# A decoder block on one core: where the partition maximum of the feed-forward weights and the sums of the skip columns stand

## The reference, cut to what matters

```
x = x + attn(layernorm(x), w_qkv, w_proj)       # 16 heads of 32, causal, ternary weights, 8-bit activations
x = x + mix(layernorm(x), k, skip, ctx, ctx)    # long convolution of products along the 512 columns, 8 x 32 grouping of positions
x = x + ffn(layernorm(x), gate, up, down)       # weights rounded to fp8 (e4m3), silu(gate) * up, then down; scales per column

mix:  kv = v[:, :, :, None, :] * x2[:, :, None, :, :]
      y  = causal_convolution(kv, k) + kv * skip
      out = einsum('bhijl,bhil->bhjl', y, x1)
ffn:  fuse = silu(q(x, gate_w) * gate_scale) * (q(x, up_w) * up_scale);  q(fuse, down_w) * down_scale
```

## Time and profile before

| | |
|---|---|
| median of three runs | 1605.58 us (1601.24, 1605.58, 1606.38) |
| the profiled execution | 1601.21 us, its span 1599.4 us |
| TensorE busy | 1479.1 us, 92% of the span |
| VectorE busy | 1261.7 us, 79% |
| GpSimd busy | 992.7 us, 62% |
| ScalarE busy | 697.4 us, 44% |
| mean granted clock of TensorE | 0.983 of full speed |

### The profile page before, as it was taken

One profiled execution on the slowest core, in us unless ns is written; L12 is line 12 of the kernel. 1 busy time (PEld: TensorE's weight loads), 2 busy tenths in 40 slices (PEclk: granted clock), 3 DMA queues, 4 the chain that ended last, 5 costly groups with the idle time before them and its releaser, 6 DMA issues.

```text
span 1599.4 us, 23982 instructions
## 1 busy us (share of the span) xinstructions
PE 1479.1 (92%) x8967; PEld 839.6 (52%) x9045; DVE 1261.7 (79%) x1841; ACT 697.4 (44%) x1222; POOL 992.7 (62%) x706
## 2 busy tenths in 40 slices
PE   2699999999876787999999999999999999999998
PEld 2477878888752333444444444444444444444443
DVE  5789999999855799888878787788778887878521
ACT  4589999999871103222222222322232223222231
POOL 2389999999973477456545654655645654566242
PEclk9799999999988999999999999999999999999999
DMA  3554645545315112000300210300030020010000
GB/s 135 154 138 132 175 136 148 159 145 144 100 59 184 42 50 77 22 7 14 79 14 9 72 27 0 79 21 7 20 80 7 14 79 14 7 40 1 1 26 27
DMA packets 58708, 105.78 MB, mean 66 GB/s; under 512 B 7625, under 2 KB 11873, under 8 KB 58593
## 3 DMA queue, kind: packets, MB, share of 16 engines
q1 hardware_dynamic: 58400, 104.10, 23.4%
q10 hardware_dynamic: 192, 0.14, 0.1%
HBM read 50.74 MB, written 19.92 MB: 44 GB/s over the span
## 4 chain that ended last, share of the span: by engine, by line
PE 61%; DVE 4%; POOL 2%; issue 1%; ACT 0%; POOLq 0%; DVEq 0%
PE gu L673 21%; PE y L638 10%; PE gu L687 10%; PE y L641 3%; PE y L646 3%; PE y L642 3%; PE gu L626 3%; PE y L645 3%; PE y L644 3%; PE misc L663 1%; PE misc L602 1%; PE misc L653 1%; PE misc L543 1%; DVE z L983 1%; DVE oT L994 1%
## 5 line engine op out<-in xcount | busy, mean ns | idle before, releaser
L1559 POOL TENSOR_TENSOR fuL<-fu,fuH 128x512 f16<-128x512 f32 x96 | 125.2, 1304 | 247.9 <-ACT fuH L1370 247.9
L638 PE MATMUL y<-kv,toep 128*128 128x512 f32 x496 | 239.8, 606 | 21.6 <-DVE z L983 19.2
L1465 POOL TENSOR_TENSOR pL<-pT,pH 128x768 f16<-128x768 f32 x128 | 216.6, 1694 | 10.9 <-ACT pH L1206 4.7
L994 DVE TENSOR_REDUCE oT<-z 128x64 f32<-128x512 f32 x256 | 175.7, 686 | 8.8
L673 PE MATMUL gu<-fT,wg 128*128 128x512 f16 x768 | 181.4, 379 | 0.3 <-ACT fT L1389 0.3
L673 PE MATMUL gu<-fT,wu 128*128 128x512 f16 x768 | 181.4, 379 | 0.0
L1370 ACT ACTIVATE fuH<-fu 128x512 f16<-128x512 f32 x96 | 60.3, 628 | 254.8 <-DVE fu L1009 254.8
L990 DVE TENSOR_TENSOR z<-z,cT 128x512 f32<-128x512 f32 x112 | 168.3, 1503 | 3.9
L987 DVE TENSOR_TENSOR z<-y,shared 128x512 f32<-128x512 f32 x112 | 76.9, 687 | 90.8 <-PE y L642 76.9
L687 PE MATMUL gu<-wd,fuH 128*128 128x512 f16 x384 | 145.5, 379 | 0.0
L687 PE MATMUL gu<-wd,fuL 128*128 128x512 f16 x384 | 145.5, 379 | 0.0
(11 more groups left out here) (188 smaller groups left out, 3392.3 us busy)
## 6 DMA issues: line engine op xcount, KB each, us to landing
pack<-qkhl SPq DMA_DIRECT2D x256, 128.0 KB, 2.4
x_sb<-in_x SPq DMA_DIRECT2D x16, 512.0 KB, 4.3
c_sb<-in_ctx SPq DMA_DIRECT2D x32, 256.0 KB, 5.0
hankel<-in_L_xattn_k SPq DMA_DIRECT2D x32, 256.0 KB, 4.4
x_grp<-x_scratch SPq DMA_DIRECT2D x32, 256.0 KB, 3.9
out_y<-yo SPq DMA_DIRECT2D x32, 256.0 KB, 2.8
x_scratch<-x_sb SPq DMA_DIRECT2D x15, 512.0 KB, 2.8
wraw<-in_L_attn_w_qkv SPq DMA_DIRECT2D x3, 1024.0 KB, 9.8
```

The costliest lines, as they stand in the source:

```text
L638: made = T.matmul(to, tap(h, lb - kb), keys_values(h, kb, half), start=kb == 0, stop=kb == lb)
L994: V.tensor_reduce(out=oT[h % 2][:, lb, own].rearrange("p (b j) -> p b j", b=HB), in_=z[n % 2][:], op=ALU.add, axis=AXIS.X).then_inc(m_z, 1)
L1465: G.tensor_tensor(pL[n % 2][:], pT[n % NP][:], pH[n % NP][:], ALU.subtract).then_inc(low_done, 1)
L1559: G.tensor_tensor(fuL[:, ib, :], fu[n % 2][:], fuH[:, ib, :], ALU.subtract).then_inc(f_fl, 1)
```

## The change

Four things move, and nothing is added or left out:

- `weight_bound` on VectorE goes from step 6 of part 2 to step 124 of part 1, one step after the last `clamp_piece`.
- `partition_all_reduce` on GpSimd goes from step 12 of part 2 to step 142 of part 1, one step after the last `sum_parts`.
- `sum_skip` on VectorE goes from step 1 of each head to step 3.
- `spread_skip` on GpSimd goes from step 2 of each head to step 4.

`fuse_bound` stays at step 20.

```diff
+        WEIGHT_BOUND_AT, REDUCE_AT = (PIECES - 1) * PAIRS + CLAMP_AT + 1, (B - 1) * PAIRS + FINISH + 1
...
-        BOUND_AT = 6, 12, 20
+        FUSE_BOUND_AT = 20
... vector_program, part 1
+            def weight_bound():
+                chain.step(V.tensor_reduce(out=mx[:, 0:2], in_=wmax[:], op=ALU.max, axis=AXIS.X))
+                w.wait_ge(tab_done, 1)
+                chain.wait()
+                V.tensor_reduce(out=mx[:, 2:4], in_=cols[:, 0:2 * IB].rearrange("p (m b) -> p m b", m=2), op=ALU.max,
+                                axis=AXIS.X, apply_absolute_value=True).then_inc(mx_done, 1)
...
                 if (n := piece(t, CLAMP_AT)) is not None:
                     clamp_piece(n)
+                if t == WEIGHT_BOUND_AT:
+                    weight_bound()
... vector_program, part 2
-                if s == 1 and h < M_HEADS:
+                if s == 3 and h < M_HEADS:
                     sum_skip(h)
...
-                if g == BOUND_AT[0]:
-                    weight_bound()
-                if g == BOUND_AT[2]:
+                if g == FUSE_BOUND_AT:
                     fuse_bound()
... gpsimd_program, part 1
                 if (n := piece(t, TAKE_AT)) is not None:
                     take_piece(n)
+                if t == REDUCE_AT:
+                    w.wait_ge(mx_done, 1)
+                    G.partition_all_reduce(mall[:], mx[:], P, RMAX).then_inc(mall_done, 1)
... gpsimd_program, part 2
-                if s == 2 and h < M_HEADS:
+                if s == 4 and h < M_HEADS:
                     spread_skip(h)
...
-                if g == BOUND_AT[1]:
-                    w.wait_ge(mx_done, 1)
-                    G.partition_all_reduce(mall[:], mx[:], P, RMAX).then_inc(mall_done, 1)
```

More of the change, by code:

```diff
@@ L1060, in down_weights @@
                     V.tensor_scalar(pw[:], pw[:], FP8_MIN_NORMAL, FP8_STEP, ALU.max, ALU.mult).then_inc(d_pow_done, 1)
[L1062 to L1067, removed]
             def fuse_bound():
```

## The result

The changed kernel takes 1597.97 us in the median of nine runs (1594.46 to 1602.28), the kernel before 1604.5 in nine: the ratio is 0.9961, 95% interval 0.9946 to 0.9976. That is 6.5 us by the medians, 6.3 by the ratio; forecast were 10.5. A second timing of it on another occasion (e8b) gave 0.9965 (0.9953 to 0.9977). So it is faster by 0.35 to 0.4%, in the stated range of 1588 to 1601 us, and by three fifths of the forecast.

A forecast was written before the change was run, and what follows sets the result against it. TensorE was taken as the bound, its end a fixed time after its unbroken stream starts at about 632 us. Gains 7.9 + 2.6 = 10.5 us gave 1595 from the median 1605.58; range 1588 to 1601.

The forecast's parts named there:

- The wait of 7.4 goes whole, GpSimd is early by 12 us: Head 2: VectorE's wait before `g_skip` (7.4 us) vanishes, since GpSimd's `kv_skip` ends 12 us earlier, 5 us to spare.
- The reduction's move is worth 9.15 - 1.25 = 7.9: Heads 1 and 2: 9.15 us of excess go, 1.25 return at `fuse_bound`; net 7.9 us, bounds 4.5 and 12.0.
- The step from the bound's place: Head 2, step 20: TensorE finds `fuse_bound` 1.25 us further in its way than before.
- the idle of 2.9 us in front of step 6: Head 2: TensorE's idle time before step 6 was to grow from 1.82 to about 3.1 us.
- the clock would not fall: Head 2: with TensorE's idle of 7.57 us gone, no half clock (0.50, 1.2 GHz) follows.
- The sum's move is worth 2.6: Head 0: statistics and next z follow about 2.8 us earlier; 2.6 us gained, bounds 0 and 2.8.
- On a path that TensorE covers: 0: Each head: VectorE's 0.69 us move from before step 1's z to before step 3's; cost 0, bounds -0.69 and +0.69.
- The reduction is free at the end of attention: End of attention: its 13.15 us fit into GpSimd's 15.74 us idle before head 0's power, 2.5 to spare; cost nothing.
- the rival of a slower load: End of attention: code loading takes 15.7 to 26 us (gain 5, chance 0.06) or 39.5 (13 slower, chance 0.04).
- mx costs 0: Part 1, step 124: two VectorE reductions of 0.2 us each fall into a 0.55 us wait; 0, bounds -0.4 and +0.4.
- Contention takes half back: Heads 2 to 4: VectorE's instructions lengthen beside GpSimd, 6 us lost; gain 4.5, 1601 us; rival, chance 0.13.
- Spreading at step 4 harms the stream: Each of 26 heads: spread_skip delays GpSimd's low parts 0.6 us, 16 against 10.5, 1611 us; rival, chance 0.02.

The follow-up runs named there:

- e8b: The changed kernel unaltered, timed and profiled a second time, against the kernel before; 1595.52 us, ratio 0.9965 (0.9953 to 0.9977).
- e9b: Against e1: GpSimd also made to wait in head 1 until TensorE's first matmul of head 2, without a reduction there; one run, 1599.27 us beside 1600.32 before.
- e1: Against the kernel before: only the reduction (with mx) moves to the end of attention, sum and spreading stay at steps 1 and 2; 1597.72 us, ratio 0.9968.
- e3: Against the changed kernel: the maximum over the partitions left out, GpSimd copies mx into mall at the same place; 1596.88 us, ratio 0.9970 to the kernel before.
- e2: Against the kernel before: only the sum and its spreading move, to steps 3 and 4, the reduction stays in head 1; ratio 1.0000.
- e4: Against the changed kernel: the bound's seven small instructions move to head 0, the down scales' one to step 7; 1593.2 us, ratio 0.9940 to the kernel before.
- e5b: Against e4: the sum at step 3 in head 0 alone, in later heads back at step 1, spreading at 2; 1591.37 us, ratio 0.9929 to the kernel before.

## Why the prediction was right, and where it was not

Direction and place held, and so did the mechanism of the larger part; the size was 10.5 us and is 6.5 (stretch) or 6.3 to 6.5 (time). That 1597.97 still lies within the forecast's own 1591.5 to 1598 is luck: the gain that went with it was 7.5 to 14, and before's median of nine came out at 1604.5, 1.1 under the 1605.58 from which the forecast had started.

- *The wait of 7.4 goes whole, GpSimd is early by 12 us.* It goes; e9b shows the hold as its cause. `kv_skip` of head 2 ends 12.7 us sooner by its distance from the first statistics (61.4 before, 48.7 changed), but only 10.2 of it is the reduction's (51.2 in e1), where 12.4 were forecast: GpSimd's own instructions took longer too when they met VectorE's, in e1 `wd` 2.33 instead of 1.27 and two `kv` 4.84 instead of 3.86. The margin was enough.
- *The reduction's move is worth 9.15 - 1.25 = 7.9.* It is 6.3 (143.0 - 136.7, e1). The step from the bound's place was well sized: head 2's step 4 to step 6 lengthens by 1.16. Two terms were missing from the sum, and these are where this part failed. Head 1's step 4 to head 2's step 2 goes from 15.2 to 16.0, since VectorE, which had been alone for 13 us, has company (0.85). And the idle of 2.9 us in front of step 6, for which I had predicted 3.1, carries a half-clock stretch: 11.7 us from step 6 to head 3's step 2 where it was 10.9 (0.83). I had written that the clock would not fall, with the idle of 7.57 in mind and not the new one. 9.15 - 1.16 - 0.85 - 0.83 = 6.3.
- *The sum's move is worth 2.6.* It is 0.2 (e1 against the changed kernel), and this is the larger error. Head 0's gain is 2.8, near the 2.6 of the forecast. "On a path that TensorE covers: 0" is the step that failed: from step 4 of one head to step 2 of the next VectorE paces heads 1 to 4 in e1 and in the changed kernel, and its 0.69 us now lie there; heads 1 to 4 give back 0.3, 1.4, 0.4 and 0.4 (e1 against changed). Head 2's 1.4 are two things. The sum ahead of the bound makes 0.86 between steps 4 and 6, where the idle grows from 2.90 to 3.86; with the bound away it is gone. The other 0.56 lie between steps 2 and 4, where heads 1 and 3 gain 0.6 by the move: in head 2 the changed kernel has a half-clock stretch there (3.40 us for four records, 1.98 in e1). The rows on which it rested spoke of TensorE's idle times before step 2, 0.99 in heads 1 and 2: releaser z, VectorE. I read them as slack of nothing; they said who paces.
- *The reduction is free at the end of attention.* Right, by e3, e1 and e8b. Its "issue" before is 5.6 to 6.1 us there, the part behind hidden, with DMA moving beside it (175 GB/s in 483 to 486 of the changed profile); the rival of a slower load did not come.
- *mx costs 0.* It stands at 436.91 and 437.18, and VectorE's wait before the next maximum shrank from 0.55 to 0.18. Right.
- *Contention takes half back,* a rival with 0.13, was near the truth in kind. By e1 it takes 0.85 of the 4.0 us that were missing, and without it the sum's new place would have cost nothing in head 1 (e2); half clock and the sum's place take the rest.
- *Spreading at step 4 harms the stream:* no. TensorE has no idle time there in the changed kernel either.
- The section before the prediction gives the busy tenths of TensorE between 480 and 640 us as 8, 7, 8 and 7; the profile's row has 6, 7, 8 and 7. Nothing was worked out from the first of them.

## What to carry to other kernels

One partition maximum shown with 0.4 us held GpSimd's in-order queue for 13 us, with a change of configuration on either side of it; put such an instruction where its engine waits anyway. And look for every neighbour in its queue, since asking later for one of them moves the wait to the next. An instruction that is moved "under the cover" of the bottleneck engine must be checked against who releases that engine in its new place: a releaser named in a row of one microsecond is the pace-maker. And whoever frees a queue should look at once for what stood next to last; here moving the bound out of head 2 too gave another 3 us (e4), and 4 with the sum moved in head 0 alone (e5b).

## What the hardware showed that I had not expected

The pause behind the partition maximum, before GpSimd's next ordinary instruction, was 6.95 us before and 7.00 in e2, more than the one ahead of it (5.6 to 6.1 in the eleven profiles that have a maximum). An instruction of VectorE on one column took 1.26 us beside GpSimd and 0.16 without; a `TENSOR_SCALAR` of 128x512 took 2.06 and 0.43, the addition of c_skip 1.69 and 0.69. z, which reads PSUM (line 983), stayed at 0.68 throughout, and so did the sum `g_skip`; the second multiplication of z (line 990), which reads none, took up to 2.3 us. TensorE's clock fell to 1.2 GHz behind an idle time of 2.90 us in e1 and did not behind one of 1.82 at the same place in the kernel before; the short half-clock stretches marked (c) and (d) came behind gaps of 1 to 2 us and moved with changes that had nothing to do with them. Executions of the changed kernel differ by up to 7.8 us; between its two profiles the whole difference arose before the first statistics, and for the others it was not measured where it arises.
